# A kernel of six graph layers: first norm in groups of 28 tiles, score stage with slope columns, batch norm turned 128 wide

## The reference, cut to what matters

```python
x_l = (x @ W_l + b_l).reshape(n, H, F); x_r = (x @ W_r + b_r).reshape(n, H, F)   # H = 4, F = 64
# edges and one own row per node (loop_attr = mean of the attributes of its incoming edges)
e_emb = (ea @ W_e).reshape(-1, H, F)
m = leaky_relu(x_l[src] + x_r[dst] + e_emb, 0.2)
alpha = einsum('ehf,hf->eh', m, att)          # the scores
# softmax of the scores over the edges of a node, weighted sum of x_l[src], mean over heads
out = out.mean(axis=1) + bias
mu = out.mean(axis=0); var = out.var(axis=0)  # batch norm over all nodes
out = gamma * (out - mu) * rsqrt(var + 1e-5) + beta
return relu(out)
```

## Time and profile before

| | us |
|---|---|
| median of 3 runs | 4874.95 (4870.29 to 4879.8) |
| profiled execution | 4874.43, of which the span 4872.4 |
| first norm | about 331 to 504 |
| score stage | about 1602 to 2438 |
| attention | about 2508 to 3118 |
| batch norm | about 3118 to 3301 |

### The profile page before, as it was taken

How to read it: one execution, slowest core, us unless ns; L and a number is a source line. 1 busy time by engine, 2 the same in 40 slices (tenths; PEclk the granted TensorE clock), 3 DMA queues, 4 the chain that set the end, 5 groups by cost and what they waited for, 6 DMA issues and landing times. The chain is left out here.

```text
span 4872.4 us, 83123 instructions
## 1 busy us (share of the span) xinstructions
PE 3738.3 (77%) x25450; PEld 3357.5 (69%) x25450; DVE 3384.4 (69%) x8271; ACT 2090.5 (43%) x5274; POOL 2879.4 (59%) x2974
## 2 busy tenths in 40 slices
PE   5720476748888799999939999895888688868888
PEld 5620466647878577777626766695888688868888
DVE  8978577766777799999968888783444344435544
ACT  6836244434444344444428888661222122212222
POOL 0001577747776677777515555447777577757775
PEclk9965687868989899999969999757888798888988
DMA  8014578756776454454423333365666466646665
GB/s 216 21 26 80 127 185 183 188 132 150 159 161 152 108 117 114 117 118 117 91 39 75 75 75 73 85 152 113 137 135 137 101 137 136 137 105 132 134 135 111
DMA packets 1646958, 583.01 MB, mean 120 GB/s; under 512 B 1549591, under 2 KB 1583254, under 8 KB 1646298
## 3 DMA queue, kind: packets, MB, share of 16 engines
q1 hardware_dynamic: 925878, 297.74, 26.9%
q10 hardware_dynamic: 636612, 195.74, 17.3%
q0 software_dynamic: 84064, 84.64, 8.7%
HBM read 381.77 MB, written 209.21 MB: 121 GB/s over the span
## 5 line engine op out<-in xcount | busy, mean ns | idle before, releaser
L2001 POOL DMA_INDIRECT early<-node_g,src_w x1173 | 1115.1, 951 | 424.4 <-issue 356.6
L2218 POOL DMA_INDIRECT early<-node_g,src_w x782 | 759.9, 972 | 297.9 <-issue 249.1
L1116 POOL DMA_INDIRECT fscat<-node_g,early x392 | 371.3, 947 | 192.5 <-issue 111.7
L2581 PE MATMUL bank<-early,faS 128*128 128x264 f32 x1568 | 375.3, 392 | 79.5 <-DVE early L2703 78.4
L2581 PEld LDWEIGHTS bank<-early,faS 128*128 128x128 f32 x1568 | 290.8, 191 | 163.0 <-issue 79.5
L1220 ACT ACTIVATE fsy<-bank 128x512 f32<-128x512 f32 x448 | 240.1, 544 | 379.0 <-DVE fslz L1265 201.3
L2262 PE MATMUL bank<-l0S,l0msg 128*128 128x128 f32 x1568 | 264.1, 346 | 165.3 <-issue 67.3
L2262 PEld LDWEIGHTS bank<-l0S,l0msg 128*128 128x128 f32 x1568 | 254.4, 258 | 172.1 <-issue 119.3
L2043 PE MATMUL bank<-l5S,l5msg 128*128 128x128 f32 x1568 | 230.5, 316 | 103.7 <-issue 68.8
L2043 PE MATMUL bank<-l3S,l3msg 128*128 128x128 f32 x1568 | 231.5, 317 | 101.8 <-issue 60.7
L2043 PE MATMUL bank<-l4S,l4msg 128*128 128x128 f32 x1568 | 229.8, 315 | 96.3 <-issue 62.1
(11 more groups left out here) (369 smaller groups left out, 10639.7 us busy)
## 6 DMA issues: line engine op xcount, KB each, us to landing
edge_h<-early SPq DMA_DIRECT2D x280, 224.0 KB
node_g<-amax ACTq DMA_DIRECT2D x224, 224.0 KB
early<-edge_h SPq DMA_DIRECT2D x168, 256.0 KB
early<-node_g,src_w POOLq DMA_INDIRECT x1955
l0msg<-edge_a ACTq DMA_DIRECT2D x56, 256.0 KB
l0msg<-edge_h SPq DMA_DIRECT2D x56, 256.0 KB
l1msg<-edge_h SPq DMA_DIRECT2D x56, 256.0 KB
alpha<-edge_h SPq DMA_DIRECT2D x56, 256.0 KB
```

The costliest lines, as they stand in the source:

```text
L1116: pool.indirect_dma_start(out=cat[:, s, t, 0:F], out_offset=None, in_=node_g, in_offset=bass.IndirectOffsetOnAxis(ap=src_i[:, col], axis=0 ...
L2001: pool.indirect_dma_start(out=ring[:, n % RING, t, :], out_offset=None, in_=table_in, in_offset=bass.IndirectOffsetOnAxis(ap=src_w[:, n * ...
L2218: pool.indirect_dma_start(out=ring[:, n % RING, t, :], out_offset=None, in_=table_in, in_offset=bass.IndirectOffsetOnAxis(ap=src_w[:, n * ...
L2581: ins = nc.tensor.matmul(bank[g % RING][:, 0:MW], S[:, s, BAND * t + q, :], M[:, s, t + q, :], start=(q == 0), stop=(q == BAND - 1))
```

## The change

Four functions are touched; what each computes stays.

1. `first_norm`: groups of 4 steps (28 tiles). The short operations and the root run once per group on 28 columns. ACT normalises 3 steps of a group whole (21 instructions), DVE the fourth (two operations of 448 columns). SP stores, in program order with its window copies, whose loop is unrolled. Four buffers, one per step of the group.
2. `edge_rows`: leaky_relu(z) = 0.2 z + 0.8 max(z, 0). Each head of the weights gets two more columns, +0.2 W att and -0.2 W att (`Wx`), so a tile has 264 columns. DVE takes max(z, 0) times (0.8 att, 1, -1) in one operation per tile out of PSUM and sums over 66. ACT's part L1220 and DVE's L1272 are gone. A bank holds one tile instead of two. For the first three tiles `near` is padded with 64 zero columns and `cat` with zeros, so that three 128-wide matmuls add up in place of a transpose to one half and two matmuls to the other. DVE's set-up grows by some 25 operations.
3. `attention`: the output's two halves are 512 and 384 columns instead of 448 and 448 (`gat_pairs`), so that a half is whole tiles. ACT's `outputs` and DVE's `moments` are two instructions each (128 x 384, 64 x 128); the aggregate at the end runs over three lists of 56 instead of two. `attention_weights` has seven more short operations.
4. `batch_norm`: ACT applies scale and shift with relu as it passes `gat_pairs` (two instructions per step), PE only turns (4 transposes per step), DVE adds (two operations per step), and the norm runs in groups of 4 steps: 2 by ACT, 2 by POOL. SP loads and, 8 steps behind, stores.

```diff
 first_norm, SP and ACT (DVE: as for batch_norm below, over GT = 28 tiles)
+                    for n in range(NS):
+                        begin = nc.sync.value_load(starts[0:1, n:n + 1], min_val=0, max_val=FRONT + NP)
                         sp.dma_start(window(dst_win, n * WR), window(dst_all, begin)).then_inc(copied, 16)
+                        q, j = n // G, n % G
+                        if j < G - 1:
+                            sp.wait_ge(g_ok, (G - 1) * q + j + 1)
+                        else:
+                            sp.wait_ge(g2_ok, q + 1)
+                        sp.dma_start(tiles(node_g[n * HS * P:(n + 1) * HS * P, :]), g[:, j, :, :]).then_inc(stored[j], 16)
...
+                    for q in range(NG):
+                        for j in range(G - 1):
+                            if j == G - 2 and q + 1 < NG:
+                                root(q + 1)
+                            rows(q, j)
...
+                    variances(0)
+                    scales(0)
+                    for q in range(NG):
+                        if q + 1 < NG:
+                            variances(q + 1)
+                        rows(q)
+                        if q + 1 < NG:
+                            scales(q + 1)
 edge_rows
-                                    nc.tensor.transpose(bank[b][0:F, col], cat[:, s, t, 0:F], ident[:, :])
+                                    nc.tensor.matmul(bank[b][:, col], cat[:, s, t, :], ident[:, :], start=True, stop=False)
                                     for w in range(SPAN):
-                                        ins = nc.tensor.matmul(bank[b][F:2 * F, col], near[:, s, t, w, :], spread[:, t, w, :], start=(w == 0), stop=(w == SPAN - 1))
+                                        ins = nc.tensor.matmul(bank[b][:, col], near[:, s, t, w, :], spread[:, t, w, :], start=False, stop=(w == SPAN - 1))
...
+                        for t in range(HS):
+                            g = block_no(n, OWN, t)
                             if g >= 4:
-                                pe.wait_ge(lz_ok, g - 3)
+                                pe.wait_ge(z_read, g - 3)
+                            nc.tensor.matmul(z_bank(g), ones_w[:, :], bias_w[:, :], start=True, stop=False)
+                            nc.tensor.matmul(z_bank(g), selfT[:, s, t * P:(t + 1) * P], flat(Wx[:, 2]), start=False, stop=True).then_inc(z_ok, 1)
...
                     def scores(n, kind):
-                        leaky(n, kind)
+                        for t in range(HS):
+                            g = block_no(n, kind, t)
+                            dve.wait_ge(z_ok, g + 1)
+                            v.scalar_tensor_tensor(prods[:, kind, t, :], z_bank(g), 0.0, attx[:, :, :].rearrange("p h f -> p (h f)"), ALU.max, ALU.mult).then_inc(z_read, 1)
+                        v.drain()
                         to = (amax, alpha)[kind][:, n * HS:(n + 1) * HS, :]
-                        v.tensor_tensor(lz[:, kind, :, :], lz[:, kind, :, :], att_ps, ALU.mult)
-                        v.drain()
-                        v.tensor_reduce(to, lz[:, kind, :, :].rearrange("p t (h f) -> p t h f", h=HEADS), AX.X, ALU.add).then_inc(scored, 1)
+                        v.tensor_reduce(to, prods[:, kind, :, :].rearrange("p t (h f) -> p t h f", h=HEADS), AX.X, ALU.add).then_inc(scored, 1)
 attention
-                        A.activation(oT[:, n % 2, :], bank[7][:, 0:HALF], ACT.Identity, bias=shift[:, 0:1], scale=1.0 / HEADS).then_inc(o_ok, 1)
+                        A.activation(oT[:, n % 2, 0:REST], bank[7][:, 0:REST], ACT.Identity, bias=shift[:, 0:1], scale=1.0 / HEADS)
+                        A.activation(oT[0:F, n % 2, REST:HALF], bank[7][0:F, REST:HALF], ACT.Identity, bias=shift[0:F, 0:1], scale=1.0 / HEADS).then_inc(o_ok, 1)
 batch_norm, SP
+                    for n in range(NS):
+                        s, at = n % SLOTS, n * UPPER * P
                         if n >= SLOTS:
-                            sp.wait_ge(turned, n - SLOTS + 1)
+                            sp.wait_ge(y_ok, n - SLOTS + 1)
+                        sp.dma_start(oT[0:F, s, :], gat_pairs[0:F, at:at + UPPER * P]).then_inc(loaded[s], 16)
+                        sp.dma_start(oT[F:2 * F, s, 0:LOWER * P], gat_pairs[F:2 * F, at:at + LOWER * P]).then_inc(loaded[s], 16)
+                        if n >= LAG:
+                            store(n - LAG)
 batch_norm, ACT
+                    def scaled(n):
+                        s = n % SLOTS
+                        act.wait_ge(loaded[s], 32 * (n // SLOTS + 1))
+                        if n >= 2:
+                            act.wait_ge(turned, n - 1)
+                        A.activation(y[:, n % 2, 0:LOWER * P], oT[:, s, 0:LOWER * P], ACT.Relu, bias=col[:, 1:2], scale=col[:, 0:1])
+                        A.activation(y[0:F, n % 2, LOWER * P:], oT[0:F, s, LOWER * P:], ACT.Relu, bias=col[0:F, 1:2], scale=col[0:F, 0:1]).then_inc(y_ok, 1)
...
+                    for n in range(G + 1):
+                        scaled(n)
                     root(0)
+                    for q in range(NG):
+                        for j in range(BY_ACT):
+                            for n in (q * G + G + 1 + 2 * j, q * G + G + 2 + 2 * j):
+                                if n < NS:
+                                    scaled(n)
+                            rows(q, j)
+                        if q + 1 < NG:
+                            root(q + 1)
 batch_norm, DVE
+                        for j in range(G):
+                            update(q * G + j)
+                            if j % 2 == 1:
+                                v.drain()
+                                for k in range((j - 1) * HS, (j + 1) * HS):
+                                    v.bn_stats(bs[:, s, k, :], x_sb[:, q * GT + k, :])
...
+                    for q in range(NG):
+                        variances(q)
+                        scales(q)
```

More of the change, by code:

```diff
@@ L2602, in outputs @@
                         for q in range(2):
-                            for half in range(2):
-                                ins = nc.tensor.matmul(bank[7][half * F:(half + 1) * F, 0:HALF], Wst[:, q, :], aggT[:, q, half * HALF:(half + 1) * HALF], start=(q == 0), stop=(q == 1))
+                            for r0, r1, c0, c1 in PARTS:
+                                ins = nc.tensor.matmul(bank[7][r0:r1, 0:c1 - c0], Wst[:, q, :], aggT[:, q, c0:c1], start=(q == 0), stop=(q == 1))
                         ins.then_inc(out_made, 1)
@@ L2791, in batch_norm @@
-                loaded, stored = many("loaded"), many("stored")
+                many = lambda name, n: [sm(f"{name}{r}") for r in range(n)]
+                SLOTS, G, LAG, BY_ACT = 4, 4, 8, 2
+                NG, GT = NS // G, G * HS
+                assert NS % G == 0
+                oT = tb("oT", [2 * F, SLOTS, UPPER * P]); y = tb("y", [2 * F, 2, UPPER * P]); col = tb("col", [2 * F, 2])
+                h = tb("h", [P, G, HS, F]); t_c = tb("t_c", [P, HS, F])
+                bs = tb("bs", [P, 2, GT, 6]); ln = tb("ln", [P, 2, 8, GT])
@@ L2801, in _ @@
+                        if n >= LAG:
+                            store(n - LAG)
+                    for n in range(NS - LAG, NS):
+                        store(n)
+                    for j in range(G):
+                        sp.wait_ge(stored[j], 16 * NG)
                 @block.tensor
                 def _(pe):
-                    pe.wait_ge(w_made, 1)
-                    nc.tensor.matmul(bank[4][0:F + 1, 0:F], turn[:, :], ident[0:F, 0:F], start=True, stop=True).then_inc(w_ps, 1)
-                    pe.wait_ge(w_ok, 1)
@@ L2846, in store @@
-                    def store(n):
-                        s = n % SLOTS
-                        act.wait_ge(h_ok, n + 1)
-                        act.wait_ge(h2_ok, n + 1)
-                        act.dma_start(tiles(node_g[nodes_of(n), :]), h[:, s, :, :]).then_inc(stored[s], 16)
-                    root(0)
-                    for n in range(NS):
-                        if n + 1 < NS:
-                            root(n + 1)
-                        if n >= 1:
-                            store(n - 1)
-                        rows(n)
@@ new lines, in root, with rows @@
+                    def root(q):
+                        act.wait_ge(var_ok, q + 1)
+                        A.activation(ln[:, q % 2, 4, :], ln[:, q % 2, 3, :], ACT.Sqrt, bias=eps[:, 0:1], scale=1.0 / F).then_inc(sd_ok, 1)
+                    def rows(q, j):
+                        if j == 0:
+                            act.wait_ge(ln_ok, q + 1)
+                        if q >= 1:
+                            act.wait_ge(stored[j], 16 * q)
+                        for t in range(HS):
+                            k = j * HS + t
+                            ins = A.activation(h[:, j, t, :], x_sb[:, q * GT + k, :], ACT.Relu, bias=ln[:, q % 2, 6, k:k + 1], scale=ln[:, q % 2, 5, k:k + 1])
+                        ins.then_inc(h_ok, 1)
@@ L2875, in variances @@
[L2875 to L2884 removed]
```

(2 more changed lines are left out.)

351 lines of the change are left out of this document (164 added, 187 removed).

## The result

The changed kernel takes 4788.6 us (median of 4 runs, 4787.53 to 4793.8) against 4874.78 (4870.29 to 4879.8): ratio 0.9823, 95% interval 0.9812 to 0.9835, 86 us less. The forecast was 4809, its range 4766 to 4848. The profiled execution has a span of 4785.6 us, 86.8 less than that of before.

What follows compares the result with a forecast made beforehand. Bounds were taken per stage: DVE in first norm and score, an ACT-DVE loop in attention, PE in batch norm. -60 - 25 + 0.5 + 12 + 1.6 + 2 + 4 = -65 from 4874.4 gave 4809, range 4766 to 4848.

Steps and rivals of the forecast that it cites:

- First norm, -60 forecast: First norm: DVE's many small instructions bound it; grouping four steps makes ACT the bound at 7.3 us per group, -60 us.
- SP ... 6.0. So ACT is late next.: First norm, per group: SP's register loads, DMAs and stores 6.0 us, DVE 6.6, ACT 7.3, so ACT is the next bound.
- rival (d): First norm: stores wait behind window copies in SP's queue, 8.2 us per group, total 4821; no chance of its own.
- Score stage, -25 forecast: Score stage: DVE relieved, PE with its four-tile ring is late next; step from 14.44 to 14.0 us, -25 us.
- Attention, +13.5 forecast: Attention: ACT's two `outputs` instructions lie on the DVE-ACT-DVE loop, 0.21 us more per step, +12; aggregate +1.6.
- Batch norm, +4 forecast: Batch norm: ACT waits each group for a load queued behind a store; group 12.4 us, 186 against 182.5, +4 us.
- L: Batch norm: time from the end of a group's second ACT step to the next load's landing, 4.3 to 5.3, taken 4.8 us.
- the lead-in and the tail: Batch norm: time outside the thirteen groups, taken as 23 us before and 14 us after.
- `attention_weights`, +2 forecast: `attention_weights`: seven more short operations on 3 partitions with drains, nothing beside them, +2 us (1 to 3).
- (a): Rival: stage bounds give way; score at POOL's 13.8, batch norm near 10.7, attention +8; total 4772, chance 0.17.
- Rival (b): New waits eat gains: score +20 (bubbles stay or weight loads exposed), batch norm L 6.5 (+22); 4872, half 4850; chance 0.22.
- (c): Rival: PE's clock falls in the score stage; at 0.89 the step is 15.6 us, +66, total 4900; chance 0.04.

Runs made afterwards that it cites:

- narrow: Changed kernel with the three expanded edge tiles turned as before (a transpose and two 64-wide matmuls instead of three padded 128-wide matmuls): 4819.43 us.
- pad_only: Kernel before with only the new turning of the three expanded edge tiles (three padded 128-wide matmuls each), VectorE and ScalarE keeping their old work: 4876.54 us.
- lag10: Changed kernel with batch norm's third loads moved two pairs later (LAG 10 instead of 8), so none stands behind the preceding pair's store: 4781.95 us.

## Why the prediction was right, and where it was not

- **First norm, -60 forecast, -55 measured.** The step that failed is "SP ... 6.0. So ACT is late next." SP took about 7.55 us per group. The store was put at the 0.4 us that ACT's queue pays, and is 0.58 on SP; register load, copy and the gap were put at 0.9 to 1.1 from the earlier trace rows, and are 1.3. The window copies stood beside the stores in one queue; the prediction did count them, and named the stores behind them as rival (d), but at 8.2 us. ACT's 7.3 was nearly right: 7.17, once SP is out of its way. The sum has a slip of 1 us: 165 - 102 - 2 is 61.
- **Score stage, -25 forecast, -23 measured.** The loop was added up right, piece by piece: 14.0 against 14.11. Even so the nearness of the totals owes something to chance: 56 steps at 0.33 us less are 18.5, not 24.6, and the rest came from the start (-3.2, the longer set-up included, which had been taken at +0.5) and the end (-1.1). The turning fell by 0.46 us a step (0.38 to 0.48 had been taken), but not for the reason given, "each tile no longer changes between half and full width": in `narrow` a half-width tile between two of its kind has the bubble too. What the prediction does not say, and `narrow` and `pad_only` show, is that neither half has a value of its own.

  The Trainium skill (TensorEngine Tiling (Array Packing), Tiling Modes), cited there, says that changing the tiling mode, not just the tile, drains the engine. The traces agree with what was concluded, six passes of full width in 0.67 us against five of half width in 0.80, but not with the ground: the bubble lies inside a tile, where all passes are of one width (128*64), and a drain at a change of mode does not account for it.
- **Attention, +13.5 forecast, +2 measured.** The step that failed is "So ACT's `outputs` lies on the loop". The instruction costs what was said (0.72 us to the next, forecast 0.73); its cover was not seen. What is left is the aggregate, 4.70 us instead of 3.18 (+1.5, forecast +1.6).
- **Batch norm, +4 forecast, -6 measured.** The mechanism is the one forecast: the load waits behind the store, and `lag10` gives back the difference to 10.7. One mis-sized term is L: 1.06 us to the second issue and 2.65 to its landing are 3.7, where 3.3 to 4.3 of landing had been read from a load of 256 KB. That second half of the load is 384 columns on 64 partitions, 96 KB, issued at 3096.10. The other is the lead-in and the tail, 23 + 14 = 37 us: from the first load to the first instruction of the next block (3038.1 to 3214.2) are 176.1 us, the thirteen groups between the first and the last root 150.0 of them (3052.0 to 3202.0), which leaves 26. And the sum has a slip that hid 12 us of this: 13 x 12.4 + 23 + 14 is 198, not 186. By its own terms batch norm was forecast at +16, 22 us too dear: 11 by the groups, 11 by lead-in and tail. That +4 stands only 10 off is luck.
- **`attention_weights`, +2 forecast.** Its seven operations aren't to be seen in the time: the first norm starts at 330.2 us against 331.2, and at 329.4 to 332.2 in all traces, with and without them.

Between the profiled executions the forecast missed by 22 us: attention 12, batch norm 10, scatter 4 and the start 3 too dear, first norm 5 and two small terms 2 too cheap. With the slip in batch norm put right the forecast is 4821, and the miss 34. The range held the time because it reached down to (a), not because (a) came: its score step of 13.8, its group near 10.7 and its +8 for attention measured 14.11, 11.5 and, without the aggregate, +0.5. Rival (b) is excluded by the turning of 2.88 us and by L = 3.7 (half of its way from 4809 to 4872 is 4840, not 4850), (c) by the clock of 1.00.

## What to carry to other kernels

A wait can sit inside a busy row: where an operation of 28 columns lasts 0.73 us and its neighbours 0.19, look for what ends at the same moment on another engine, and do so over many steps, before an engine is put on the critical loop. When two engines stand within a per cent of each other, price the halves of an edit together, since each alone gave nothing here, and ask for the third (here GpSimd's gathers, 0.4 us below). Add a forecast up once more from its own terms before it is used, for an error of addition can hide an error of measure. A queue that only issues DMAs is an engine too: its rows are short, and what it costs is the distance from one to the next.

## What the runs showed of the hardware that was not expected

- The operation of DVE with two inputs in SBUF that meets POOL's addition of 768 columns ends 0.03 to 0.06 us after it in 77 steps of two traces, at lengths of 0.73 and 0.53 us in the median; without the meeting it takes 0.19. A one-input operation inside the same addition is not lengthened.
- A store of one step costs 0.38 us to issue when no other issue stands right ahead of it in its queue, on SP (3095.07) as on ACT (L1908 and L2850 of the kernel before, 0.38 in the median), and 0.58 when it comes 0.05 us after another DMA's issue on SP (398.40). Over the 4 stores of a group that is 0.8 us, more than the 0.4 by which SP's group stood above ACT's.
- Six passes of full width are 0.13 us faster than five of half width that go to two halves of a bank (0.67 against 0.80 us a tile), also where the tiles on both sides have the same half width.
